# Gathered rows turned by VectorE behind a pass through DRAM, instead of by TensorE

## The chip, the cores and the metric

One Trainium2 chip; the kernel runs on one of its cores. The metric is device time in microseconds (us), the median of several executions. The engines are named as in the profile: PE is TensorE (PEld its weight loads), DVE is VectorE, ACT is ScalarE, POOL is GpSimd, SP is SyncE, which only starts DMAs here.

## What is computed

A layer in two stages over 4 x 512 tokens of width 512. The first is a state-space block; its result is added to x. The second is a mixture of experts: after a layer norm each token takes its best 6 of 16 experts, and all tokens also pass a shared one.

```python
def _swiglu(x, w13_, w2_):
    gu = x @ w13_.T
    g, u = jnp.split(gu, 2, axis=-1)
    return jax.nn.silu(g) * u @ w2_.T
...
scores = jax.nn.softmax(x @ gate_w.T, axis=-1)
topk_w, topk_ids = lax.top_k(scores, TOP_K)
topk_w = topk_w / (topk_w.sum(-1, keepdims=True) + 1e-20)
combine = jnp.einsum('tk,tke->te', topk_w, jax.nn.one_hot(topk_ids, E, dtype=topk_w.dtype))
...
out, _ = lax.scan(body, jnp.zeros_like(x), (w13, w2, combine.T))
out = out + _swiglu(x, sw13, sw2)
```

H = 512, I = 352, E = 16, TOP_K = 6; the shared expert has 2 x 352 inner columns.

## The kernel before

The program is written by hand for each engine; semaphores order the engines among each other, and each engine runs its own list in order. The first stage is left as it is but for a few constants; the second is what the change is about.

**Weights and tiles.** There are 18 weight sets of 2.2 MB: two halves of the shared expert (sets 0 and 1) and 16 experts (2 to 17). A tile is 128 tokens through one set. 32 tiles are shared ones (t < NS = 32), and here 104 routed ones follow, 6 to 7 per expert, in a loop of four tiles per turn. A routed tile's tokens are scattered rows of `token_rows`.

**Precision.** Each operand of the matmuls is taken as a high part plus a low part: `xh` is a copy of x into a narrower type, `xl = x - xh`; likewise `ah`, `al` of the middle result, and for the weights `w` (high) and w's second half (low, `wraw - w`). Three products (high x high, high x low, low x high) are summed.

**One routed tile, by engine.** `tile(t)` on PE: `up` of the chunks 0 and 1 (L1699, L1700), `turn_a(t-1)` (L1710), `up` of the chunks 2 and 3, `turn_x(t+1)` (L1687: four 128x128 transposes of the gathered rows into bank 4), `down(t-1)` (L1719). ACT: `a_high(t-1)` (L862), `x_high(t+1)` (L852, reads bank 4), `gate_up(t)` (L857), `y_out(t-1)` (L868). DVE: `a_low(t-1)` (L1399), `take_weight(t+1)` (L1372), `gather_ids(t+5)` (L1378), `x_low(t+1)` (L1363: bank 4 minus xh), `add_ids` (L1383), `multiply(t)` (L1393). POOL: `gather(t+5)` (L997), `next_weights(t)`, `expert_starts(t)`, `add(t)` (L1015, adds 128 rows into the output in DRAM). Shared tiles read rows that were stored turned, so they have no `turn_x`.

**A split.** At an expert's first tile the next set's parts are made: ACT (L822) and DVE (L1417) copy half of `wraw` each into the high part, then POOL's `split_low` (L987) subtracts all 4352 columns. The set after that is fetched by SP (L633) into the one `wraw` when L987 is done. There are 15 splits in the routed stage.

**The passage to the routed tiles.** POOL loads the token lists (L1060) after tile 26; DVE waits for them (`ids_in`) ahead of tile NS-3 = 29, where the first `gather_ids` stand (`FIRST_ROWS`).

Of the kernel before, what the change touches and what calls it, by code (L numbers as in the profile page):

```python
# [37 lines left out]
P = 128  # L38
# [24 lines left out]
SHARE = WCOLS // 2  # L63
PEELED = NS - 1
AHEAD = 5
FIRST_ROWS = {NS - 3: (NS, NS + 1), NS - 2: (NS + 2,), NS - 1: (NS + 3, NS + 4)}
# [165 lines left out]
def mamba_moe(nc, x, ctxT, g_x, g_f, inT, convw, convb, xpT, dtwT, dtb, alog, dvec,  # L232
# [4 lines left out]
    turned_d = nc.dram_tensor("token_rows_turned", (TT, P, H), F32, kind="Internal").ap()  # L237
    turned_v = turned_d.rearrange("(b c) p m -> b p c m", c=TC)
# [6 lines left out]
    with ExitStack() as ctx:  # L245
# [49 lines left out]
        dskm = alloc(mem, "dskm", [P, J, P])  # L295
# [8 lines left out]
        u1 = alloc(mem, "u1", [P, J, L])  # L304
        hs = alloc(mem, "hs", [P, 4, L])
        hc = alloc(mem, "hc", [P, 4, L])
        xlT = alloc(mem, "xlT", [P, TC, HK, P])
        szT = alloc(mem, "szT", [P, TC, H])
# [16 lines left out]
        zero = alloc(mem, "zero", [P, ROW])  # L325
# [33 lines left out]
        wraw = alloc(ctx, "wraw", [P, WCOLS])  # L359
        w = alloc(ctx, "w", [P, 4 * WCOLS], F32R)  # L360


        sg = alloc(ctx, "sg", [P, 2, I])
# [4 lines left out]
        xh = alloc(ctx, "xh", [P, 2, H], F32R)  # L368
        xl = alloc(ctx, "xl", [P, 2, H], F32R)
# [5 lines left out]
        meta = alloc(ctx, "meta", [P, 5, NT], I32)  # L375
# [13 lines left out]
        fours = alloc(ctx, "fours", [P, 2], I32)  # L389
# [57 lines left out]
        gathered = [sem(f"gathered{i}") for i in range(4)]  # L447
        zero_done = sem("zero_done")
# [31 lines left out]
        N_CONST = 10  # L480
# [30 lines left out]

        def tiles_but_12(eng):
            return eng.value_load(fours[0:1, 1:2], min_val=NS + E - 12, max_val=TILES - 12)
# [4 lines left out]
        def up_banks(t, s):  # L518

            return misc if isinstance(t, int) and t == 0 else banks[2 * s:2 * s + 2]  # L520

# [19 lines left out]
        def _(sp):  # L541
# [3 lines left out]
                      (gf, g_f.partition_broadcast(P)), (dsk, dvec.rearrange("(j p) -> p j", p=P)), (iota16, iota_d),  # L545
                      (gw, gateT.rearrange("(k p) e -> p k e", p=P))]
            sp.dma_start(ctxt[:], ctxT[bass.ds(0, 1)].rearrange("a (k p) t -> p (a k) t", p=P)).then_inc(ctx_in, 16)
            with nc.allow_non_contiguous_dma(reason="per-channel vectors of 512 values"):
                for dst, src in lead:
                    sp.dma_start(dst[:], src).then_inc(lead_in, 16)  # L550
                for dst, src in consts:
                    sp.dma_start(dst[:], src).then_inc(const_in, 16)
# [31 lines left out]
            def step(b, at):  # L584
# [7 lines left out]
                if b == NB - 1 and n == 2:  # L592
                    sp.wait_ge(dA_done, b * DS * J)
                    sp.wait_ge(g_done, b * DS)
                    sp.wait_ge(summed, (b - 1) * DS * J + J * J)
                    fetch(0)
# [33 lines left out]
            def fetch(e):  # L630

                at_least(sp, wl_done, e)
                sp.dma_start(wraw[:], wall[bass.ds(e, 1)].rearrange("a p c -> p (a c)")).then_inc(raw_in, 16)  # L633
# [24 lines left out]
            with sp.Fori(3, NX) as e:  # L658
                fetch(e)
            sp.wait_ge(meta_ready, 2)  # L660
            tiles = tiles_but_12(sp) + 12
# [5 lines left out]
        def _(act):  # L667
# [92 lines left out]
            def norm_chunk(b, t):  # L760
                act.wait_ge(nmr2_done, b + 1)
                act.wait_ge(rows_stored, 16 * (b + 1))
                nc.scalar.activation(rowb[:, t, 0:H], xrow[:, b % 2, t, :], ACT.Identity, bias=nmr2[:, t:t + 1],
# [52 lines left out]
            def split_high(e, t):  # L816
# [3 lines left out]
                apart(act, raw_in, 16 * (e + 1), "act")  # L820
                apart(act, down_done, t, "act")
                nc.scalar.copy(columns(w, (e % 2) * 2 * WCOLS, mine), wraw[:, 0:mine]).then_inc(wh_done, 1)  # L822

            def high(b, k):
                if k == 0:
                    act.wait_ge(raw_in, 16)
# [10 lines left out]
            def fetch(e):  # L837

                act.wait_ge(wl_done, e)
                act.dma_start(wraw[:], wall[bass.ds(e, 1)].rearrange("a p c -> p (a c)")).then_inc(raw_in, 16)  # L840

            def x_high(t, s):
# [5 lines left out]
                else:  # L848
                    act.wait_ge(xt_turned, t + 1)
                    source = banks[4][:]  # L850
                at_least(act, up_done, t - 1)
                nc.scalar.copy(xh[:, s, :], source).then_inc(xh_done, 1)  # L852
# [28 lines left out]
            def high_piece(e, k):  # L881
                size, base = WCOLS // EARLY, (e % 2) * 2 * WCOLS
                at = k * size
                if k == 0:
                    act.wait_ge(raw_in, 16 * (e + 1))
# [935 lines left out]
```

## Time and profile before

| | |
|---|---|
| median of 3 runs | 1438.2 us (1437.75 to 1438.47) |
| span of the profiled execution (its own time isn't given) | 1435.5 us |
| PE busy | 1349.9 us (94%) |
| POOL, DVE, ACT busy | 949.3, 787.5, 730.9 us |
| DMA | 149 MB, 104 GB/s |
| second stage | from about 490 us to the end |

The profile gives busy times per engine, the granted clock of TensorE, the chain of waits that ended last, groups of instructions by source line, and timelines. The line numbers are those of the kernel before. Matmuls overlap, so the sum of their times is more than the time that they take.

### The profile page before, as it was taken

To read this page: it belongs to the slowest core of one execution; us is meant where nothing else is said; L and a number is where in the kernel's file an instruction comes from. 1 tells how busy PE (TensorE), PEld (TensorE's weight loads), DVE (VectorE), ACT (ScalarE), POOL (GpSimd) and SP (SyncE) were. 2 spreads that over 40 slices of the span, in tenths; PEclk is the share of its full clock that TensorE was granted. 3 is DMA by queue.
4 is the path that set the end of the run, shared out by engine and by line. 5 is a ranking of instruction groups with operands and counts; after the bars stand their busy time and mean duration, and the time that the engine had idled before them with its cause. 6 is when DMAs were issued, how large, how long until landed. Compare 5 with 4: busy or idle time off the path is not lost.

```text
span 1435.5 us, 32257 instructions
## 1 busy us (share of the span) xinstructions
PE 1349.9 (94%) x8480; PEld 1210.6 (84%) x8481; DVE 787.5 (55%) x1364; ACT 730.9 (51%) x1317; POOL 949.3 (66%) x671
## 2 busy tenths in 40 slices
PE   6897998997898899999999999999999999999996
PEld 2686887887888799999998989989889988899885
DVE  6878898898989854653333333333333333333331
ACT  5898897898889464343332333323333333332321
POOL 0588898898988747887456665566645666546632
PEclk8899999999999999999999999999999999999999
DMA  4120122222242365645455435555445544454432
GB/s 137 38 74 31 53 67 96 67 73 91 75 146 72 133 129 106 142 84 141 83 141 145 131 63 144 139 147 137 104 94 137 141 135 104 95 147 131 76 68 36
DMA packets 65042, 149.13 MB, mean 104 GB/s; under 512 B 16976, under 2 KB 17616, under 8 KB 62656
## 3 DMA queue, kind: packets, MB, share of 16 engines
q0 software_dynamic: 31024, 62.10, 22.9%
q1 hardware_dynamic: 33392, 81.21, 17.5%
q10 hardware_dynamic: 560, 4.98, 1.0%
q8 instruction: 36, 0.59, 0.2%
q14 instruction: 30, 0.25, 0.1%
HBM read 101.50 MB, written 48.99 MB: 105 GB/s over the span
## 4 chain that ended last, share of the span: by engine, by line
PE 65%; DVE 3%; issue 1%; POOL 0%; ACT 0%; DVEq 0%; POOLq 0%; ACTq 0%
PE bank L1719 19%; PE bank L1699 19%; PE bank L1700 18%; PE bank L1687 3%; PE bank L1710 3%; DVE hs L1172 1%; PE bank L1604 1%; PE bank L1590 1%; PE bank L1602 0%; POOL hc L949 0%; DVE sc L1226 0%; PE bank L1665 0%; DVEq L1375 0%; DVE xl L1363 0%; DVE du L1186 0%
## 5 line engine op out<-in xcount | busy, mean ns | idle before, releaser
L949 POOL TENSOR_TENSOR hc<-hs,crow 128x512 f32<-128x512 f32 x254 | 322.6, 1302 | 91.8 <-DVE hs L1172 84.6
L1699 PE MATMUL bank<-w,xh 128*128 (+1 forms) x1088 | 368.7, 340 | 7.6 <-issue 4.2
L1015 POOL DMA_INDIRECT out_x<-ys,aid x104 | 171.2, 1646 | 275.0 <-issue 215.7
L1700 PE MATMUL bank<-w,xh 128*128 (+1 forms) x1088 | 351.2, 323 | 0.0
L1172 DVE TENSOR_TENSOR_SCAN hs<-dA,bank 128x512 f32<-128x512 f32 x256 | 295.8, 1208 | 47.9 <-PE bank L1604 32.0
L1719 PE MATMUL bank<-w,ah 128*128 (+1 forms) x816 | 264.7, 405 | 2.7 <-DVE al L1399 2.7
L1399 DVE TENSOR_TENSOR al<-bank,ah 128x384 fp32r<-128x384 f32 x136 | 75.8, 557 | 331.0 <-ACT ah L862 283.2
L1699 PEld LDWEIGHTS bank<-w,xh 128*128 128x128 f32 x1088 | 204.3, 188 | 35.9 <-issue 32.1
L1700 PEld LDWEIGHTS bank<-w,xh 128*128 128x128 f32 x1088 | 206.4, 190 | 2.3
L868 ACT COPY ys<-bank 128x512 f32<-128x512 f32 x136 | 79.9, 587 | 195.9 <-PE bank L1719 191.5
L1700 PE MATMUL bank<-w,xl 128*128 (+1 forms) x544 | 175.9, 323 | 0.0
L1699 PE MATMUL bank<-w,xl 128*128 (+1 forms) x544 | 175.7, 323 | 0.0
L1719 PEld LDWEIGHTS bank<-w,ah 128*128 128x128 f32 x816 | 145.0, 189 | 27.7 <-issue 2.2
L1590 PE MATMUL bank<-ident,hc 128*128 128x128 f32 x1024 | 160.4, 281 | 7.6 <-POOL hc L949 5.1
L862 ACT CAST ah<-bank 128x384 fp32r<-128x384 f32 x136 | 65.3, 480 | 196.9 <-PE bank L1710 166.7
L786 ACT ACTIVATE dA<-delta,aneg 128x512 f32<-128x512 f32 x256 | 164.0, 710 | 0.0
L1604 PE MATMUL bank<-bdiag,duT 128*128 128x128 f32 x1024 | 163.7, 285 | 0.0
L1719 PE MATMUL bank<-w,al 128*128 (+1 forms) x408 | 161.2, 395 | 0.0
L852 ACT CAST xh<-bank 128x512 fp32r<-128x512 f32 x104 | 61.2, 588 | 182.9 <-PE bank L1687 175.4
L987 POOL TENSOR_TENSOR w<-wraw,w 128x4352 f32 x15 | 143.8, 9588 | 0.7 <-issue 0.5
L1604 PEld LDWEIGHTS bank<-bdiag,duT 128*128 128x128 f32 x1024 | 142.5, 201 | 0.0
L1590 PEld LDWEIGHTS bank<-ident,hc 128*128 128x128 f32 x1024 | 124.3, 145 | 11.0 <-POOL hc L949 6.7
(184 smaller groups left out, 2051.7 us busy)
## 6 DMA issues: line engine op xcount, KB each, us to landing
wraw<-in_wall SPq DMA_DIRECT2D x16, 2176.0 KB
crow<-c_rows SPq DMA_DIRECT2D x64, 256.0 KB, 3.3
xt<-token_rows_turned SPq DMA_DIRECT2D x32, 256.0 KB
out_x<-ys POOLq DMA_DIRECT2D x32, 256.0 KB
wraw<-in_wall ACTq DMA_DIRECT2D x2, 2176.0 KB
token_rows<-rowb SPq DMA_DIRECT2D x4, 1028.0 KB
xrow<-in_x SPq DMA_DIRECT2D x4, 1024.0 KB, 7.0
out_x<-xrow SPq DMA_DIRECT2D x4, 1024.0 KB, 4.9
```

The lines of the kernel that those rows point to most:

```text
L786: nc.scalar.activation(dA[:, 4 * (n % 2) + j, :], delta[b % 2][:, j, :], ACT.Exp, scale=aneg[:, j, n:n + 1]).then_inc(dA_done, 1)
L868: nc.scalar.copy(ys[:, slot, :], banks[7][:]).then_inc(ys_done, 1)
L949: nc.gpsimd.tensor_tensor(hc[:, j, :], hs[:, j, :], crow[:, n % 4, :], ALU.mult).then_inc(hc_done, 1)
L987: nc.gpsimd.tensor_tensor(columns(w, at + WCOLS, WCOLS), wraw[:], columns(w, at, WCOLS), ALU.subtract).then_inc(wl_done, 1)
L1015: pool.indirect_dma_start(out_rows, bass.IndirectOffsetOnAxis(ap=aid[:, s:s + 1], axis=0), ys[:, s, :], None, bounds_check=TOKENS - 1, oob ...
L1172: nc.vector.tensor_tensor_scan(hs[:, j, :], dA[:, 4 * (n % 2) + j, :], dbu[j % 2][:], 0.0, ALU.mult, ALU.add).then_inc(scanned, 1)
L1399: nc.vector.tensor_tensor(al[:, s, :], banks[5][:, 0:IP], ah[:, s, :], ALU.subtract).then_inc(al_done, 1)
L1590: mm = nc.tensor.matmul(ysum[t][:, cols], hc[:, j, t * P:(t + 1) * P], ident[:], start=n == 0 and j == 0, stop=n == DS - 1, is_transpose=T ...
L1604: mm = nc.tensor.matmul(dbu[j % 2][:, t * P:(t + 1) * P], duT[b % 2][:, t, j * P:(j + 1) * P], bdiag[:, n % 2, t - COPIED, :], start=True, ...
L1699: nc.tensor.matmul(gate_bank[:, 0:I], xx, columns(w, off + ww + k * 2 * I, I), start=first, stop=last)
L1700: mm = nc.tensor.matmul(up_bank[:, 0:I], xx, columns(w, off + ww + k * 2 * I + I, I), start=first, stop=last)
L1719: mm = nc.tensor.matmul(banks[7][:], aa, columns(w, off + ww + W2AT + k * H, H), start=k == 0 and n == 0, stop=k == IK - 1 and n == 2)
```

## The change

- A routed tile's rows, gathered into `xt` as before, are stored to DRAM (`gathered_rows`) by SP, 256 KB, and read back by SP in four DMAs, one for each quarter of the partitions: partition 32q + r of `xq` gets, for each of four groups of 32 tokens, 128 columns (512 B) of a token.
- DVE's STREAM_TRANSPOSE (`turn_x`, first in its tile) turns each 32x32 block of `xq` into `xsq`; `x_high` and `x_low` read `xsq`, blockwise, where they read bank 4. PE's `turn_x` is gone.
- So that blocks fall where the matmuls want them, the normed rows are written in another order of columns, and the sets 0 and 1 and the gate's weights are loaded in that order (five and four DMAs instead of one).
- `wraw` has two halves. From set 4 on a set is fetched by ACT's queue, right behind ACT's copy of the set before (`fetch_after`), where SP waited for L987.
- The first gathers stand one tile earlier: from tile NS-4 = 28 on, with the wait for `ids_in`.
- SP stores a tile's rows one tile ahead of reading back: store of t+1, then the four reads of t.

```diff
-FIRST_ROWS = {NS - 3: (NS, NS + 1), NS - 2: (NS + 2,), NS - 1: (NS + 3, NS + 4)}
+FIRST_ROWS = {NS - 4: (NS, NS + 1), NS - 3: (NS + 2,), NS - 2: (NS + 3,), NS - 1: (NS + 4,)}
+ROWS_FROM = min(FIRST_ROWS)
...
+            def bounce_out(t, s, m=None):
+                rows_in(sp, t, s, m, "sp")
+                apart(sp, xt_turned, t - 3, "sp")
+                sp.dma_start(bounce_d[s], xt[:, s, 0:H]).then_inc(bounced[s], 16)
+            def bounce_in(t, s, m=None):
+                apart(sp, bounced[s], 16 * ((t - NS) // 4 + 1) if isinstance(t, int) else 16 * m + 16, "sp")
+                apart(sp, xt_turned, t - 3, "sp")
+                for q in range(NQ):
+                    sp.dma_start(xq[q * Q:(q + 1) * Q, s, :].rearrange("r (g f) -> r g f", g=NQ), quarter_v[s, q]).then_inc(quartered[s], 16)
...
-            with sp.Fori(3, NX) as e:
-                fetch(e)
+            fetch(3)
             sp.wait_ge(meta_ready, 2)
+            groups = routed_groups(sp)
+            bounce_out(NS, 0)
+            with sp.Fori(0, groups - 1) as i:
+                for k in range(4):
+                    t = 4 * i + NS + k
+                    bounce_out(t + 1, (k + 1) % 4, i + (k + 1) // 4)
+                    bounce_in(t, k, i)
...
+            def fetch_after(e, t):
+                apart(act, wl_done, e, "act")
+                late = act.value_load(meta[0:1, 5, bass.ds(t, 1)], min_val=0, max_val=NX - 1)
+                act.dma_start(columns(wraw, ((e + 1) % 2) * WCOLS, WCOLS),
+                              wall[bass.ds(late, 1)].rearrange("a p c -> p (a c)")).then_inc(raw_in, 16)
...
                 with act.If(e > 0):
                     split_high(e, t)
+                    fetch_after(e, t)
...
-                    apart(pool, xt_turned, t - 3, "pool")
+                    apart(pool, bounced[s], 16 * ((t - NS) // 4 if isinstance(t, int) else before), "pool")
...
+            def turn_x(t, s4, m=None):
+                if isinstance(t, int) and t < NS:
+                    return
+                quarters_in(dve, t, s4, m, "dve")
+                apart(dve, xl_done, t, "dve")
+                nc.vector.transpose(xsq[:], xq[:, s4, :]).then_inc(xt_turned, 1)
...
-                source = xt[:, t % 4, 0:H] if isinstance(t, int) and t < NS else banks[4][:]
-                nc.vector.tensor_tensor(xl[:, s, :], source, xh[:, s, :], ALU.subtract).then_inc(xl_done, 1)
+                if isinstance(t, int) and t < NS:
+                    nc.vector.tensor_tensor(xl[:, s, :], xt[:, t % 4, 0:H], xh[:, s, :], ALU.subtract).then_inc(xl_done, 1)
+                else:
+                    dve.wait_ge(xt_turned, t + 1)
+                    nc.vector.tensor_tensor(xl[:, s, :].rearrange("p (c g r) -> p c g r", c=NQ, r=Q),
+                                            xsq[:].rearrange("p (g c r) -> p c g r", g=NQ, r=Q),
+                                            xh[:, s, :].rearrange("p (c g r) -> p c g r", c=NQ, r=Q), ALU.subtract).then_inc(xl_done, 1)
...
                 s = s4 % 2
+                turn_x(t + 1, (s4 + 1) % 4, m)
                 a_low(t - 1, 1 - s)
...
-                if t == NS - 3:
+                if t == ROWS_FROM:
                     dve.wait_ge(ids_in, 16)
...
-                if more and not (isinstance(t, int) and t + 1 < NS):
-                    turn_x(t + 1, (s4 + 1) % 4, m)
```

VectorE, one routed tile in the loop, behind the split's branch; before (cc is the token's weight, gid the next gather's indices):

```order
L1399 TENSOR_TENSOR al<-bank,ah 128x384
...
L1372 COPY cc<-xt 128x1
...
L1378 COPY gid<-lists 128x1
L1360 REGISTER_ALU
L1363 TENSOR_TENSOR xl<-bank,xh 128x512
```

and in the change (its own line numbers):

```order
L1450 STREAM_TRANSPOSE xsq<-xq 128x512
L1497 TENSOR_TENSOR al<-bank,ah 128x384
...
L1470 COPY cc<-xt 128x1
...
L1476 COPY gid<-lists 128x1
L1453 REGISTER_ALU
L1459 TENSOR_TENSOR xl<-xsq,xh 128x512
```

The transpose stands ahead of al, and x_low, at its old place behind gid, reads xsq where it read a bank.

SyncE behind the last shared rows; before:

```order
L658 UNCONDITIONAL_BRANCH
L633 ISA
L633 DMA wraw<-in_wall 128x4352
L658 REGISTER_ALU
L658 COMPARE_AND_BRANCH
```

and in the change, the first two tiles of the loop's turn:

```order
L684 DMA gathered_rows<-xt 128x512
L720 UNCONDITIONAL_BRANCH
L720 ISA
L500 ISA
L684 DMA gathered_rows<-xt 128x512
L500 REGISTER_ALU
L691 DMA xq<-gathered_rows 32x4x128 x4
L500 REGISTER_ALU
L684 DMA gathered_rows<-xt 128x512
L691 DMA xq<-gathered_rows 32x4x128 x4
```

The fetches of weights have left the loop; the reads of a tile stand behind the store of the next one.

## Rows read from the trace of the kernel before

**Rows 1.** The page's first line.

```profile
span 1435.5 us, 32257 instructions
```

**Rows 2.** Busy time by engine in a window: PE, PEld, DVE, ACT, POOL; clock, DMA share, GB/s.

```profile
450.00:1400.00 950.00, 936.22 (x5548) 856.23 (x5548) 396.34 (x893) 344.12 (x617) 586.09 (x381) 1.00 0.50 118
```

**Rows 3.** The chain in order of time (start, us, what): two shared, then routed tiles.

```profile
644.05 0.33 PE bank L1710 x3
...
650.35 0.33 PE bank L1710 x3
...
677.78 2.09 PE bank L1719 x9
...
722.55 0.33 PE bank L1710 x3
...
729.29 0.33 PE bank L1710 x3
```

**Rows 4.** TensorE's line 1687: count, ns min/median/max, first and last start.

```profile
L1687 PE MATMUL bank<-ident,xt x416: 270/272/273, 697.0 to 1410.1; 128*128 128x128 f32 x139
```

**Rows 5.** Timeline of DVE: an ordinary tile's al; then a split's gid and x_low.

```profile
1006.54 0.56 DVE L1399 TENSOR_TENSOR al<-bank,ah 128x384 fp32r<-128x384 f32 x1 [2.24 <-ACT ah L862]
...
1023.06 0.15 DVE L1378 COPY gid<-lists 128x1 int32 x1 [0.68 <-issue]
1023.24 0.69 DVE L1363 TENSOR_TENSOR xl<-bank,xh 128x512 fp32r<-128x512 f32 x1
```

**Rows 6.** Timeline of POOL in the same split, and the gather behind it.

```profile
1022.79 9.58 POOL L987 TENSOR_TENSOR w<-wraw,w 128x4352 f32 x1
...
1034.44 0.99 POOL L997 DMA_INDIRECT xt<-token_rows,gid  x1 [0.30 <-issue]
```

**Rows 7.** Lines 1150, 1363 and 987, columns as in rows 4.

```profile
L1150 DVE TENSOR_TENSOR delta<-delta,du x16: 681/1080/1769, 27.6 to 365.1; 128x512 f32<-128x512 f32 x16
...
L1363 DVE TENSOR_TENSOR xl<-bank,xh x104: 690/692/693, 698.2 to 1411.1; 128x512 fp32r<-128x512 f32 x104
...
L987 POOL TENSOR_TENSOR w<-wraw,w x15: 9564/9587/9625, 711.1 to 1342.3; 128x4352 f32 x15
```

**Rows 8.** Timelines of DVE and POOL around one of the 16 L1150.

```profile
119.64 1.42 DVE L1150 TENSOR_TENSOR delta<-delta,du 128x512 f32<-128x512 f32 x1
...
119.25 1.27 POOL L949 TENSOR_TENSOR hc<-hs,crow 128x512 f32<-128x512 f32 x1
```

**Rows 9.** Timelines: x_low of the first, ninth and last split; POOL's L987 of the ninth.

```profile
712.23 0.69 DVE L1363 TENSOR_TENSOR xl<-bank,xh 128x512 fp32r<-128x512 f32 x1
...
1071.92 0.69 DVE L1363 TENSOR_TENSOR xl<-bank,xh 128x512 fp32r<-128x512 f32 x1
...
1342.96 0.69 DVE L1363 TENSOR_TENSOR xl<-bank,xh 128x512 fp32r<-128x512 f32 x1
...
1072.21 9.59 POOL L987 TENSOR_TENSOR w<-wraw,w 128x4352 f32 x1
```

**Rows 10.** Timeline of PE: the first up matmul behind that split.

```profile
1024.96 0.43 PE L1699 MATMUL bank<-w,xh 128*128 x1 [0.64 <-issue]
```

**Rows 11.** Windows as in rows 2: an idle TensorE, and what follows.

```profile
440.70:445.40 4.70, 0.00 (x0) 0.00 (x0) 4.56 (x16) 4.70 (x10) 2.04 (x2) 1.00 0.24 52
445.60:448.90 3.30, 3.30 (x16) 3.30 (x17) 2.17 (x2) 3.29 (x4) 3.30 (x3) 0.50 0.00 1
```

**Rows 12.** Timelines of POOL and DVE at tile 28.

```profile
678.11 0.59 POOL L1060 DMA_DIRECT2D lists<-token_lists  x1 [0.47 <-DMA token_lists<-ids,posi]
...
676.40 0.56 DVE L1399 TENSOR_TENSOR al<-bank,ah 128x384 fp32r<-128x384 f32 x1 [3.79 <-issue]
```

**Rows 13.** DMA issues: count, KB each, median us to landing; one issue of SP's.

```profile
lists<-token_lists POOLq DMA_DIRECT2D x1, 136.0 KB, 3.8
...
ones<-in_ones_d SPq DMA_DIRECT2D x1, 64.0 KB, 2.7
...
25.56 0.43 SPq L628 DMA_DIRECT2D ones<-in_ones_d  x1
```

More of the change, by code:

```diff
@@ L388, in mamba_moe @@
         lasti = alloc(ctx, "lasti", [P, 1], I32)
-        fours = alloc(ctx, "fours", [P, 2], I32)
+        fours = alloc(ctx, "fours", [P, 3], I32)
+        xq = alloc(ctx, "xq", [P, 4, H])
+        xsq = alloc(ctx, "xsq", [P, H])
         lead_in = sem("lead_in")
@@ L447, in mamba_moe @@
         gathered = [sem(f"gathered{i}") for i in range(4)]
+        bounced = [sem(f"bounced{i}") for i in range(4)]
+        quartered = [sem(f"quartered{i}") for i in range(4)]
         zero_done = sem("zero_done")
@@ L479, in mamba_moe @@
         N_WARM = 4
-        N_CONST = 10
+        N_CONST = 13
         N_PLAN = 7
@@ L520, in up_banks, with raw_of, raw_count, load_raw @@
             return misc if isinstance(t, int) and t == 0 else banks[2 * s:2 * s + 2]
+        def raw_of(e):
+            return 0 if isinstance(e, int) and e < 3 else (e % 2) * WCOLS
+        def raw_count(e):
+            return 16 * (NQ + 1) * (e + 1) if isinstance(e, int) and e < 2 else 16 * e + 16 * (2 * NQ + 1)
+        def load_raw(eng, e):
+            into = columns(wraw, raw_of(e), WCOLS)
+            if e > 1:
+                eng.dma_start(into, wall[e]).then_inc(raw_in, 16)
+                return
+            parts = wall[e][:, 0:W2AT].rearrange("(q r) (c m) -> c r q m", r=Q, c=NQ)
+            for c in range(NQ):
+                eng.dma_start(into[c * Q:(c + 1) * Q, 0:W2AT].rearrange("r (q m) -> r q m", q=NQ), parts[c]).then_inc(raw_in, 16)
+            eng.dma_start(into[:, W2AT:WCOLS], wall[e][:, W2AT:WCOLS]).then_inc(raw_in, 16)
+        def by_part(a):
+            return a.rearrange("p (q c r) -> p c q r", q=NQ, r=Q)
         def split(e, k, pieces):
@@ L657, in _ @@
                 x_load(t)
-            with sp.Fori(3, NX) as e:
-                fetch(e)
+            fetch(3)
             sp.wait_ge(meta_ready, 2)
+            groups = routed_groups(sp)
[5 more added lines that the diff above has]
+                    bounce_in(t, k, i)
+            rest, rounds = tiles_but_12(sp) + 8, groups_but_2(sp) + 1
+            for k in range(4):
+                if k < 3:
+                    bounce_out(rest + k + 1, k + 1, rounds)
+                bounce_in(rest + k, k, rounds)
             tiles = tiles_but_12(sp) + 12
@@ L1065, in _ @@
                     t = 4 * i + NS + k
-                    gather(t + AHEAD, (k + AHEAD) % 4)
+                    gather(t + AHEAD, (k + AHEAD) % 4, i + (k + AHEAD) // 4)
                     next_weights(t)
@@ L1725, in weights_of, with tile @@
                 apart(pe, wl_done, needed, "pe")
-                return pe.value_load(meta[0:1, 1, bass.ds(t, 1)], min_val=0, max_val=2 * WCOLS)
-            def tile(t, s4, old, off, more=True, m=None):
+                return pe.value_load(meta[0:1, 1, bass.ds(t, 1)], min_val=0, max_val=4 * WCOLS)
+            def tile(t, s4, old, off):
                 s = s4 % 2
@@ L1769, in of_last @@
             def of_last(k):
-                return pe.value_load(meta[0:1, 1, bass.ds(last - k, 1)], min_val=0, max_val=2 * WCOLS)
-            tile(last, 3, lambda: of_last(1), weights_of(last), False)
+                return pe.value_load(meta[0:1, 1, bass.ds(last - k, 1)], min_val=0, max_val=4 * WCOLS)
+            tile(last, 3, lambda: of_last(1), weights_of(last))
             turn_a(last, 1)
```

105 lines of the change are left out of this document (61 added, 44 removed).

## The prediction

> **What bounds the kernel now.** Look first at the busy times of the routed stage: from 450 to 1400 us TensorE works 936 of 950 us, at a granted clock of 1.00, while VectorE has work for 396 us, ScalarE for 344 and GpSimd for 586 [rows 2]. So the second stage is TensorE's, and an instruction taken off it counts in full, as long as nobody comes late. Then the chain in order of time: a shared tile, which turns no rows on TensorE, takes 650.35 - 644.05 = 6.30 us; a routed tile, which does, takes 729.29 - 722.55 = 6.74 [rows 3]. The difference, 0.44 us, is what the four transposes of line 1687 cost on the path; there are 416 of them, 104 tiles' worth [rows 4]. Third, the timeline of VectorE and GpSimd around one split (the step in which a new expert's weights become a high and a low part): GpSimd's subtraction L987 runs from 1022.79 for 9.58 us, and VectorE's x_low L1363 starts at 1023.24, under it, and still takes 0.69 [rows 5, 6]. It reads a bank and xh. That row carries the prediction.
>
> The profiled execution spans 1435.5 us [rows 1]; its own time is not on the page, and the runs' median of 1438.2 is 2.7 above the span. I put these 2.7 around the changed span too, so sums start from 1438.2. A difference of 0.2%, 2.9 us, is about what can be told from no change here.
>
> **The change, part by part.**
>
> *TensorE's transposes go.* 104 x 0.44 = 45.8 us off the path.
>
> *The turning on VectorE comes.* One STREAM_TRANSPOSE of 128x512 per routed tile, ahead of al. No such row exists; al takes 0.56 and x_low 0.69 [rows 5], so I take 0.65, between half and twice that. It stands where VectorE sits idle 2.24 us before al [rows 5]: nothing on the path, at 1.3 us neither. If a quarter lands late this cover turns into a wait, and al, x_low and then TensorE's down are queued behind it (rivals).
>
> *x_low changes its inputs.* It now reads xsq and xh, both in SBUF. Take VectorE's delta L1150, which also reads two SBUF tensors. Alone it takes 0.68 us; among GpSimd's multiplications up to 1.77 [rows 7]. Case by case: GpSimd's L949 runs 119.25 to 120.52, L1150 starts at 119.64 inside it and ends at 121.06, 0.54 after GpSimd's end [rows 8]. I went through the 11 that began inside a GpSimd multiplication: each ends about 0.55 after that one's end and none earlier. The x_low of before never pays this: 690 to 693 ns in all 104 [rows 7], with a bank as its other input. So the new x_low, if it starts under L987, waits for L987's end. It does: in the first split x_low starts at 712.23 and L987 at 711.1, in the last at 1342.96 and 1342.3; in 14 of 15 x_low is 0.4 to 1.2 us behind. Only the one at 1071.92 is ahead of its L987, by 0.29 [rows 7, 9]. The change doesn't bring x_low forward, since it starts right behind gid, not behind TensorE's turning (gid from 1023.06, x_low from 1023.24 [rows 5]), and L987 starts right behind a gather in both kernels. Price: L987 ends at 1032.37, x_low 0.55 later at 1032.92; the tile's first matmul, at 1024.96 before [rows 10] and 0.44 earlier without the turning, starts at about 1032.97. That is 8.45 us; in the first split the same working gives 8.1. I take 8.4, so 14 x 8.4 = 117.6. In the fifteenth the next tile's x_low is held instead, for the last 3 us: 3. Sum 120.6. Behind it all stand multiply, TensorE's up and everything of the next tile; nothing else fills TensorE.
>
> The longest wait that a row shows is 1.77 - 0.68 = 1.09 us, behind an instruction of 1.27; whether it also lasts 9 us behind one of 9.58, no row shows. Bounds: 1.1 us, of which x_low's spare hides most (it ended at 1023.93, 0.6 us ahead of the moved-up matmul), and the full remainder. I take the full one, because all the ends follow GpSimd's end and none its start. The Trainium skill ("SBUF — State Buffer", section "SBUF: two separate sides") has a rule on exactly this: VectorE with two SBUF inputs and a GpSimd instruction that reads SBUF share a pair of ports, and whichever starts first has it "for the whole instruction". By that rule each split pays the full remainder, as in my sum; with a hold of 1.1 us at most, 15 splits would cost about 8 us and the kernel would stand at rival 2.
>
> *The clock.* After an idle TensorE of 440.7 to 445.4 the granted clock was 0.50 from 445.6 to 448.9 [rows 11], the lower of its two levels (1.2 against 2.4 GHz), and half of these 3.4 us is lost: 1.7. An idle of 8 us per split has no row; I take 1.7 for each of the 14 (bounds 0 and 2.8): 23.8.
>
> *The first gathers move one tile forward.* VectorE now waits for ids_in ahead of tile 28. The load of lists is issued at 678.11 and lands 3.8 later, at 681.9; tile 28's al stood at 676.40 [rows 12, 13]. It slips by 5.5, to an end at 682.6, and down, which started at 677.78 [rows 3], by 4.8: with what follows al I take 5 us, once, and 1.7 of clock.
>
> *The way through DRAM.* 104 x (256 KB out, 256 KB back): 512 KB per tile beside DMA engines that are busy half of the time [rows 2]. SyncE issues five DMAs per tile at 0.43 each [rows 13], 2.2 us in a period of 6.3. In a tile without a split this all fits into the lead of the gathers; costed at nothing. The cover is two tiles of lead. The other weight sets come by ScalarE's queue right behind its copy, with GpSimd's subtraction still to run, so about 10 us earlier than SyncE's (which waited for L987): nothing on the path. The five pieces of set 0 and 1 and three more constants are issued while those queues wait anyway: nothing.
>
> **Sum:** 1438.2 - 45.8 + 120.6 + 23.8 + 6.7 = 1543.5; I say 1543. This case's own range: 13 full holds of 8.1 and no loss of clock, 1438.2 - 45.8 + 5 + 105 + 6 = 1508; 15 of 8.5 with 2.8 of clock each, 1438.2 - 45.8 + 7 + 170 = 1570.
>
> **Rivals.**
>
> 1. *x_low slips in front of the subtraction.* If the wait for a tile's turning is gone and VectorE gets 0.4 to 1.2 us ahead, all splits go like the one at 1071.92: the next tile's x_low waits about 3 us, with 1.7 of clock. 1438.2 - 40.8 + 15 x 4.7 = 1468. Against it: x_low hangs on gid, whose place is unchanged.
>
> 2. *The hold is short, and the kernel is faster.* What decides then is the gather behind a split. It is issued at 1034.44, since GpSimd was in L987 until 1032.37 [rows 6]. Landing as the lists do, 3.8, gives 1038.2; the pieces of the tile before are issued only behind this tile's store (SyncE's order), so the last of four starts 1.8 later and lands 2.7 after that, as `ones`, the same 512 B per partition, did [rows 13]: 1042.7. Turning, al and down (0.65 + 0.56 + 2.1 [rows 3], with 0.1 between) put the next tile at 1046.1; it was due three periods behind 1024.52, at 1043.4. So 2.7 us per split, 40 in all, which cancels 45.8 - 5. The kernel is faster by more than a measurement needs only if the pieces land before about 1042.5. With the four landing 3.3 behind the gather instead of 4.5, the splits cost 1.5 each: 1438.2 - 40.8 + 22 = 1420. For it: nothing shows a 9.6 us hold. Against: no row shows VectorE let in before GpSimd's end.
>
> 3. *The hold is short and the pieces are late*, by the traffic they add: 4 us per split, 1438.2 - 40.8 + 60 = 1457. About equal, if the estimate of rival 2 holds as it stands.
>
> **How the numbers follow.** Forecast 0.80, rival 1 0.06, rival 2 0.07, rival 3 0.07 (0.03 of it within 0.2%). The time is the forecast's. From 1465 to 1575 the range takes in rival 1 and nearly all of the forecast's own 1508 to 1570; rivals 2 and 3, 0.14, stay out with a few hundredths of tails. Faster 0.07, same 0.03, slower 0.90.
>
> **What would show it.** Right: x_low with a mean far over 0.69, 14 or 15 of them near 9.5 us, each ending 0.5 us after a subtraction; no turning on TensorE and 6.3 us per tile elsewhere; in each split an idle TensorE of 8 us ended by x_low, the clock at 0.5 after it; one wait of 5 us at tile 28. Wrong: x_low at 0.7 throughout (then look for VectorE's turning waiting for quarters five tiles into each expert, and TensorE idle before down), or a clock that stays at 1.0, which alone would bring the time to about 1518.

## The result, and the profile after

The changed kernel takes 1583.1 us (median of 4 runs, 1580.2 to 1584.8) against 1438.0 for the kernel before beside it: a ratio of 1.102, 95% interval 1.100 to 1.103. The forecast was 1543, its range 1465 to 1575. Its direction and its main mechanism hold; the time lies 8 us outside.

The first lines to read are the page's: the span, VectorE's x_low with a mean of 1922 ns where all 104 took 0.69 before [rows 7], and up's first line, ahead of which TensorE idled 141.9 us, 131.6 of it ended by x_low.

```profile
span 1578.4 us, 32970 instructions
...
L1792 PE MATMUL bank<-w,xh 128*128 (+1 forms) x1088 | 387.4, 357 | 141.9 <-DVE xl L1459 131.6
...
L1459 DVE TENSOR_TENSOR xl<-xsq,xh 128x512 fp32r<-128x512 f32 x104 | 199.9, 1922 | 5.9
```

The window that answers to [rows 2] is 140 us longer, and TensorE has no more to do in it: 938 us in 1090, at a granted clock of 0.93.

```profile
450.00:1540.00 1090.00, 938.05 (x5127) 842.25 (x5127) 589.62 (x992) 347.58 (x617) 585.43 (x381) 0.93 0.60 155
```

Now a split, in the timelines of VectorE, GpSimd and TensorE. x_low (L1459) starts 1.14 us behind the subtraction and ends at 1100.67, 0.56 behind the subtraction's end (1100.11); multiply, TensorE's up and all else stand behind it.

```profile
1091.62 0.15 DVE L1476 COPY gid<-lists 128x1 int32 x1 [0.69 <-issue]
1091.84 8.83 DVE L1459 TENSOR_TENSOR xl<-xsq,xh 128x512 fp32r<-128x512 f32 x1
...
1090.70 9.41 POOL L1069 TENSOR_TENSOR w<-wraw,w  x1
...
1100.90 0.66 PE L1792 MATMUL bank<-w,xh 128*128 x1 [8.04 <-DVE xl L1459]
```

In all 15 splits x_low takes 8.51 to 10.08 us and ends 0.55 or 0.56 behind the subtraction; TensorE's 15 idles there sum to 126.0 us (7.75 to 9.18). The windows behind that split (columns as in [rows 2]) show the clock at its lower level, 0.50 and 0.51, from 1095.7 to 1106, over the rest of the idle and the first 5.1 us of work after it (1.60 + 3.50); from 1106 to 1112 it is at 1.00.

```profile
1095.70:1102.50 6.80, 1.60 (x5) 1.60 (x6) 6.14 (x4) 0.00 (x0) 6.33 (x3) 0.50 0.48 145
1102.50:1106.00 3.50, 3.50 (x14) 3.43 (x14) 0.00 (x0) 0.47 (x2) 0.91 (x1) 0.51 0.83 149
```

An ordinary routed tile stands next (VectorE, then TensorE). From one turn_a (L1803) to the next such a tile takes 6.74 us in the median, without any turning on TensorE.

```profile
1055.65 0.56 DVE L1497 TENSOR_TENSOR al<-bank,ah 128x384 fp32r<-128x384 f32 x1 [1.27 <-ACT ah L942]
1056.62 0.15 DVE L1470 COPY cc<-xt 128x1 f32 x1 [0.41 <-issue]
1058.11 0.15 DVE L1476 COPY gid<-lists 128x1 int32 x1 [1.34 <-issue]
1058.32 0.69 DVE L1459 TENSOR_TENSOR xl<-xsq,xh 128x512 fp32r<-128x512 f32 x1
...
1059.31 0.43 PE L1792 MATMUL bank<-w,xh 128*128 x1 [0.17 <-issue]
```

And tile 28, in the chain in order of time: the lists' load, al, down.

```profile
678.45 3.20 DMA lists<-token_lists
...
681.98 0.57 DVE al L1497
682.59 3.91 PE bank L1812 x9
```

A tile's length is read from one start of turn_a to the next in TensorE's timeline (L1710 before, L1803 after). Over the routed stage that gives the whole difference (one such step per tile; a split's step is the one in which its subtraction starts):

| part | before | after | difference | forecast |
|---|---|---|---|---|
| 15 tiles with a split | 7.46 each | 16.80 each | +140.1 | +137.8 (120.6 + 23.8 - 15 x 0.44) |
| tile 28 | 6.29 | 12.49 | +6.2 | +6.7 |
| the 90 other steps | 615.3 in all | 611.5 | -3.8 | -39.2 (89 x 0.44) |
| sum | | | +142.5 (spans: +142.9) | +105.3 |

So the splits came about as forecast, and the gain did not come. Of the 90 other steps 15 are the next behind a split (101.3 us in all before, 106.0 after); the 75 that are left, the ordinary steps below, went from 514.0 to 505.5, a mean of 6.85 and 6.74. Two questions were left: is it really the hold, and why is a tile without transposes no shorter?

### The profile page after: what moved, and what is told of

It reads as the page before. It is cut to its first block, busy times and chain, and to the rows that moved or that the text cites. A ratio compares the mean times of both kernels' runs of the same rounds, so it can differ in the third digit from the quotient of the medians.

```text
span 1578.4 us, 32970 instructions
## 1 busy us (share of the span) xinstructions
PE 1356.9 (86%) x8064; PEld 1199.0 (76%) x8065; DVE 981.7 (62%) x1470; ACT 734.6 (47%) x1317; POOL 949.2 (60%) x671
## 4 chain that ended last, share of the span: by engine, by line
PE 45%; DVE 12%; issue 5%; DVEq 4%; POOL 4%; ACTq 2%; ACT 2%; DMA 0%; POOLq 0%
PE bank L1792 14%; PE bank L1793 13%; PE bank L1812 12%; DVE xl L1459 9%; POOL token_lists L1109 3%; PE bank L1803 2%; DVEq L1473 2%; DVEq L1467 1%; DVE hs L1255 1%; ACT ah L942 1%; PE bank L1704 1%; PE bank L1690 1%; POOL out_x L1091 1%; ACTq L897 0%; PE bank L1702 0%
## 5 line engine op out<-in xcount | busy, mean ns | idle before, releaser
L1792 PE MATMUL bank<-w,xh 128*128 (+1 forms) x1088 | 387.4, 357 | 141.9 <-DVE xl L1459 131.6
L1793 PE MATMUL bank<-w,xh 128*128 (+1 forms) x1088 | 362.7, 334 | 0.0
L1792 PEld LDWEIGHTS bank<-w,xh 128*128 128x128 f32 x1088 | 216.5, 199 | 186.6 <-issue 184.2
L1812 PE MATMUL bank<-w,ah 128*128 (+1 forms) x816 | 259.0, 399 | 7.6 <-DVE al L1497 7.3
L1793 PEld LDWEIGHTS bank<-w,xh 128*128 128x128 f32 x1088 | 215.7, 198 | 1.4
L1459 DVE TENSOR_TENSOR xl<-xsq,xh 128x512 fp32r<-128x512 f32 x104 | 199.9, 1922 | 5.9
L1792 PE MATMUL bank<-w,xl 128*128 (+1 forms) x544 | 181.3, 333 | 0.0
L1793 PE MATMUL bank<-w,xl 128*128 (+1 forms) x544 | 181.2, 333 | 0.0
L1812 PEld LDWEIGHTS bank<-w,ah 128*128 128x128 f32 x816 | 150.1, 189 | 36.0 <-issue 6.3
L1069 POOL TENSOR_TENSOR w<-wraw,w x15 | 140.9, 9393 | 0.5 <-issue 0.2
```

The source lines that it names most:

```text
L1069: nc.gpsimd.tensor_tensor(columns(w, at + WCOLS, WCOLS), columns(wraw, raw_of(e), WCOLS), columns(w, at, WCOLS), ALU.subtract).then_inc(wl ...
L1459: nc.vector.tensor_tensor(xl[:, s, :].rearrange("p (c g r) -> p c g r", c=NQ, r=Q), xsq[:].rearrange("p (g c r) -> p c g r", g=NQ, r=Q), x ...
L1792: nc.tensor.matmul(gate_bank[:, 0:I], xx, columns(w, off + ww + k * 2 * I, I), start=first, stop=last)
L1793: mm = nc.tensor.matmul(up_bank[:, 0:I], xx, columns(w, off + ww + k * 2 * I + I, I), start=first, stop=last)
L1812: mm = nc.tensor.matmul(banks[7][:], aa, columns(w, off + ww + W2AT + k * H, H), start=k == 0 and n == 0, stop=k == IK - 1 and n == 2)
```

## The experiments

All times are medians; the kernel before, measured beside each, was at 1435.9 to 1437.8, and every ratio is to it. Where an expectation speaks of the first run, that is the one with the turned rows in a bank; the third is the one with x_low ahead of gather_ids, the fourth has both. "Tile behind the split" is the next step after the split's own, 7.07 us in the changed kernel.

**The hold alone, in the kernel before.**

```
-                source = xt[:, t % 4, 0:H] if isinstance(t, int) and t < NS else banks[4][:]
+                source = xt[:, t % 4, 0:H] if isinstance(t, int) and t < NS else blank[:]
```

> The kernel before the change, with one operand of x_low moved: in routed tiles it subtracts xh from a blank tile in SBUF (zeros) instead of from the bank, so the low part of x is left out of what is computed; size, place and everything else stay. This is the hold alone, without the way through DRAM and without ScalarE's weight queue. Lead theory (two SBUF inputs shut out by GpSimd's 9.6 us subtraction): x_low at 8 to 10.5 us in all 15 splits, each split 8.5 to 9.5 us longer, so 1437 + 128 to 143 = 1565 to 1580 us. Rival (in the changed kernel the hold hid behind, or was made by, late rows, and by itself costs little): under 1500.

Measured 1588.2 us, ratio 1.105 (1.103 to 1.107). Line 1364, the moved x_low (duration ns min/median/max, then who waited for it):

```profile
L1364 DVE TENSOR_TENSOR xl<-blank,xh x104: 691/693/10218, 698.3 to 1562.6; 128x512 fp32r<-128x512 f32 x104
...
  PE bank L1701: 128.1, 15
```

Fifteen waits, 128.1 us; the split's step is 17.11, 9.65 more than before. The time is 8 us above the expected range, x_low's 8.78 to 10.22 us are within theirs. One operand's place makes a loss as large as the whole change's, with no other part of it. The lead theory stands.

**The turned rows in a bank.** STREAM_TRANSPOSE writes PSUM bank 4, which x_high and x_low read.

```
-                nc.vector.transpose(xsq[:], xq[:, s4, :]).then_inc(xt_turned, 1)
+                nc.vector.transpose(banks[4][:], xq[:, s4, :]).then_inc(xt_turned, 1)
```

> Only the place of the turned rows changes: VectorE's STREAM_TRANSPOSE writes PSUM bank 4, so x_low has one SBUF input again. Lead theory (x_low with two SBUF inputs is shut out for the whole of GpSimd's 9.4 us subtraction): x_low takes 0.69 to 0.72 us in all 104 tiles, the tile behind a split falls from 16.8 to 6.5 to 8.5 us, and with 15 splits at 8.3 to 10 each less the time falls by 125 to 150, to 1433 to 1458 us; ordinary tiles stay at 6.7. Rival (the 9 us at a split come from something else that the change brought there, the way through DRAM or ScalarE's weight DMA behind its copy): the splits stay at 14 us or more, and the time above 1550.

Measured 1502.9, ratio 1.046 (1.044 to 1.047). x_low is free again in all tiles, and the split's step is 7.18. But only 80 us came back, not 140: the tile behind the split went from 7.07 to 11.13 (15 x 4.06 = 61). The lines of x_low and of STREAM_TRANSPOSE with what VectorE waited for, the chain at one such tile, and ScalarE's weight DMA:

```profile
L1459 DVE TENSOR_TENSOR xl<-bank,xh x104: 690/692/694, 705.5 to 1478.0; 128x512 fp32r<-128x512 f32 x104
...
L1450 DVE STREAM_TRANSPOSE bank<-xq x104: 714/726/729, 701.0 to 1473.7; 128x512 f32<-128x512 f32 x104
...
  DMA xq<-gathered_rows: 144.3, 52
...
1109.58 9.24 DMA xq<-gathered_rows
...
1108.39 0.36 ACTq L897 DMA_DIRECT2D wraw<-in_wall  x1
```

Quarters issued 1.2 us behind a weight set took 9.2 us to land. In the changed kernel VectorE waited 11.2 us for quarters in 10 places, here 144.3 in 52: the hold had hidden a second wait.

**The subtraction in eight pieces.**

```
+                for k in range(8):
+                    c = k * (WCOLS // 8)
+                    low = nc.gpsimd.tensor_tensor(columns(w, at + WCOLS + c, WCOLS // 8), ...
```

> Only GpSimd's subtraction changes: eight instructions of 544 columns instead of one of 4352. Lead theory (x_low waits for the end of the GpSimd instruction in whose run it starts): no x_low takes more than about 2.5 us (one piece of 1.2 us, twice at most, and 0.7), the tile behind a split falls from 16.8 to about 8 to 9 us, and the time by 15 x 8, to 1455 to 1485. Rival 1 (VectorE is let in only when GpSimd's whole row of instructions is through): x_low stays at 8.5 us or more at the splits, the time at 1575 to 1595. Rival 2 (it is not this sharing at all): also no change.

Measured 1589.9, ratio 1.106 (1.104 to 1.108): rival 1. GpSimd's eight pieces (one row here) and x_low:

```profile
1096.39 10.35 POOL L1071 TENSOR_TENSOR w<-wraw,w  x8
...
1096.50 10.79 DVE L1462 TENSOR_TENSOR xl<-xsq,xh 128x512 fp32r<-128x512 f32 x1
```

VectorE was not let in between back-to-back instructions in 14 splits; in the first one it was, behind one piece (x_low 1.15 us). Nor do instructions in a row always shut it out: in the first stage of the kernel before, 10 of the 11 L1150 that began inside a multiplication were let in at its end, though the next one followed at once. The one behind [rows 8] took 1.72 us in place of 1.27:

```profile
120.47 1.72 POOL L949 TENSOR_TENSOR hc<-hs,crow 128x512 f32<-128x512 f32 x1
```

What differs isn't shown. The rows show this much: in the 14 splits GpSimd's gather ends 0.03 us or less ahead of the first piece, in the first split 0.29 us.

**x_low ahead of gather_ids.**

```
-                elif gathers:
-                    gather_ids(t + AHEAD, (s4 + 1) % 4)
                 x_low(t + 1, 1 - s)
+                if gathers:
+                    gather_ids(t + AHEAD, (s4 + 1) % 4)
```

> Only VectorE's order in a routed tile changes: x_low goes ahead of gather_ids (a register load and the gid copy, some 1.5 us), whose result GpSimd needs a tile later. Lead theory (the tile without the turning on TensorE is bound by VectorE's row al, cc, register load, gid, x_low): x_low ends 1 to 1.5 us earlier, ordinary routed tiles fall from 6.7 to 6.3 us, some 75 to 88 of them, 31 to 37 us in all. At the splits x_low then starts ahead of GpSimd's subtraction in many cases, and the next tile's is held for its last 1 to 3 us: 15 x 5 to 8 less. In all 1583 - 34 - 100 = 1450, between 1420 and 1490; if x_low still starts behind the subtraction, 1525 to 1550. Rival (the tile is held at 6.7 by rows that land or are turned late): tiles stay at 6.7 and the gain, if any, comes from the splits alone.

Measured 1576.6, ratio 1.093 (1.086 to 1.100). Both halves of the expectation missed. At the splits x_low now starts ahead of the subtraction and is held all the same:

```profile
1092.00 10.58 DVE L1459 TENSOR_TENSOR xl<-xsq,xh 128x512 fp32r<-128x512 f32 x1
...
1092.65 9.37 POOL L1069 TENSOR_TENSOR w<-wraw,w  x1
```

Twelve that started 0.37 to 0.66 us ahead lost; one that started 0.15 ahead took 0.69, and there the subtraction took 9.95; one was through before the subtraction began, and one began behind it. In all twelve GpSimd's gather was still running when x_low began, and the subtraction followed it within 0.03 us; where 0.15 was enough (the first split again) GpSimd was idle for 0.48 us ahead of the subtraction. A gather alone held none: 60 other x_low beside one took 0.69 to 0.71. And ordinary steps stayed at 6.75 in the median, though x_low ends early. VectorE's x_low, then TensorE:

```profile
1064.60 0.69 DVE L1459 TENSOR_TENSOR xl<-xsq,xh 128x512 fp32r<-128x512 f32 x1
...
1067.14 0.43 PE L1792 MATMUL bank<-w,xh 128*128 x1 [0.23 <-issue]
```

TensorE still idles 0.23 us, 1.85 us after x_low. So something of TensorE's own stands there. Its sequencer's rows name it: two loads of a register per tile (weights_of), which come behind down's wait for al. In the changed kernel (PEldq is the sequencer; count, ns min/median/max, first and last start):

```profile
L1817 PEldq TENSOR_LOAD <-meta x105: 297/385/933, 697.5 to 1554.2; - x105
...
L1819 PEldq TENSOR_LOAD <-meta x105: 294/302/591, 698.4 to 1555.1; - x105
```

That gives a round of waits for one tile: turn_a, a_high, al, the loads, up's first two chunks, the next turn_a. Medians over the ordinary tiles of the changed kernel: 1.60 us from turn_a's start to al's end, 3.10 to the next up, 2.04 to the next turn_a, 6.74 in all. In the kernel before they are 1.60, 3.20 and 2.00, 6.80 in all; in the tile whose al stands in [rows 5], al ends at 1007.10 and the next up starts 3.38 us later:

```profile
1010.48 0.43 PE L1699 MATMUL bank<-w,xh 128*128 x1
```

Beside the middle part TensorE had the transposes and down to work on before, and has only down now, but the round is as long.

**Both rows of register loads.** Three kernels with the turned rows in the bank: x_low ahead of gather_ids; TensorE's two values for the next tile read early, ahead of turn_a and of down, in three tiles of four; and both.

```
                 up(t, s, (0, 1), off)
+                if needed_next:
+                    needed_next()
                 turn_a(t - 1, 1 - s)
...
                 up(t, s, (2, 3), off)
+                if offset_next:
+                    offset_next()
```

> The changes of the first and the third run together: turned rows in bank 4, and x_low ahead of gather_ids. Lead theory (hold at the splits and VectorE's order in the tile are what took the gain): x_low 0.7 us everywhere, ordinary tiles 6.3, splits 6.5 to 8, so 1583 - 140 - 36 = 1407, between 1395 and 1430, which is below the kernel before the change (1438). Rival (the pieces that come through DRAM arrive late behind each split, 1.5 to 4.5 us each, as worked out from the kernel before): 1430 to 1470, with VectorE's STREAM_TRANSPOSE waiting for quarters some five tiles into each expert.

> The first run (bank 4) and TensorE's early register values, without the move of x_low. If VectorE's row (al, cc, register load, gid, x_low, which ended 4.39 us behind the start of turn_a) is a second limit of the same length, ordinary tiles stay at 6.6 to 6.75 and the time at 1493 to 1503 us; if TensorE's register values were the only limit, this comes out as the run with both, at 1470 to 1480.

> The fourth run (bank 4, x_low ahead of gather_ids) and one thing more: TensorE reads the next tile's two register values (expert and weight offset) ahead of turn_a and of down, in three tiles out of four; the first tile of each four reads them where it did. What is to be told apart is why ordinary routed tiles stay at 6.7 us though x_low now ends more than 1 us earlier. Theory A (TensorE's queue stands at down until al is there, and only then reads the registers for the next tile, 2.8 to 3.1 us from the end of al to the next matmul, where 2.1 us of down is the only work): three of four ordinary tiles fall to 6.3, one stays at 6.6 to 6.7, 75 tiles by about 0.3 to 0.4, so 1470 to 1480 us. Theory B (the limit is something else, such as ScalarE or the DMA): all stay near 6.7, 1495 to 1505.

Measured 1501.5, 1508.0 and 1505.6 (ratios 1.044, 1.050, 1.047, each to within 0.002): no gain in time in any, and all three outside the ranges expected (the one with both by 0.6 us). But the tiles tell the causes apart. Of 105 steps, 6.36 us or less took: in the bank kernel 0, with x_low moved 0, with TensorE's values early 18, with both 39. Four starts of turn_a in a row in the one with both, 6.30 and 6.31 apart:

```profile
1126.58 0.49 PE L1803 MATMUL bank<-ident,am 128*128 128x128 f32 x3
...
1132.88 0.49 PE L1803 MATMUL bank<-ident,am 128*128 128x128 f32 x3
...
1139.19 0.49 PE L1803 MATMUL bank<-ident,am 128*128 128x128 f32 x3
...
1145.50 0.49 PE L1803 MATMUL bank<-ident,am 128*128 128x128 f32 x3
```

TensorE's loads are the first limit, VectorE's row the second. The time did not follow since the rows come no faster: with both, VectorE waits 156.3 us for quarters, in 60 places.

**The same in the changed kernel, hold and all**, where rows have time to catch up at each split; TensorE's loop turns over in the middle of a tile, so all four tiles read early.

```
+                    turn_a(t - 1, 1 - s)
+                    needed = pe.value_load(meta[0:1, 0, bass.ds(t + 1, 1)], min_val=1, max_val=NX)
+                    up(t, s, (2, 3), off)
+                    following = offset_of(t + 1)
+                    down(t - 1, 1 - s, old)
+                    apart(pe, wl_done, needed, "pe")
+                    up(t + 1, 1 - s, (0, 1), following)
```

> The changed kernel with nothing done against the hold (turned rows stay in SBUF), but with both register moves: x_low ahead of gather_ids, and TensorE's register values for the next tile read while it has work queued, in all four tiles. The hold gives the rows 9 us of extra lead at each split, so here the supply of rows should not stand in the way. If the two rows of register loads are what kept ordinary tiles at 6.7 us, most of the 74 tiles between the splits fall to 6.31 to 6.4: 1583 - 74 x 0.35 = 1557 us, between 1545 and 1565, or less where an x_low slips by the subtraction. If the supply of rows limits them even behind a hold, tiles of 6.31 stand beside tiles of 7 and more, with VectorE waiting for quarters in more than 30 tiles, and the time stays above 1568.

Measured 1555.0, ratio 1.080 (1.077 to 1.082): 28 us less, as expected, but not from the ordinary tiles alone. In two of the 15 splits of the profiled execution x_low slipped by (steps of 6.95 and 7.07), as in two of the run with x_low moved alone; together with the steps behind them the splits give 12.6 us. The 75 ordinary steps give 15.5: 490.0 us in all, median 6.37 (6.74 in the changed kernel). Forty of the 105 steps are at 6.36 or less (none there). The round is now 1.60 + 2.80 + 1.94 = 6.34. Against the run with x_low moved alone (1576.6), in which the same two splits were free, TensorE's loads are the only difference, and they give 21.6 us. VectorE waits 44.0 us for quarters in 35 places, the sign of a short supply of rows, so that is no longer wholly out of the way. From the kernel before, the 75 ordinary steps now gain 24.0 of the 33 us that 75 x 0.44 would be: this is where most of the gain went.

**The rows' way through DRAM.** Four kernels on the bank kernel. First, the weight set as two DMAs of four strided pieces, so 2176 B in a row in place of 17408:

```
+                for h in range(2):
+                    act.dma_start(into[:, :, h, :], source[:, :, h, :]).then_inc(raw_in, 16)
```

> The first run (turned rows in bank 4) and one thing more: a weight set is fetched by two DMAs of rows cut into four pieces of 544 columns, so packets of 2176 B in place of 17408 B; bytes, queue and place are the same. What is to be told apart is why the tile two behind a split took 9.4 to 13.5 us (mean 11.1) there, with VectorE's STREAM_TRANSPOSE waiting for quarters that were issued about 9 us before. Theory A (the quarters' 512 B packets each stand behind a 0.65 us packet of the weight set on the same DMA engine): that tile falls to 7 to 8.5 us, the time by 15 x 2.5 to 4, to 1440 to 1465 us. Theory B (the gather is late because GpSimd was in its subtraction, and the pieces follow it, as worked out from the kernel before): the tile stays at 10 us or more and the time at 1495 to 1510.

Measured 1489.9, ratio 1.036 (1.032 to 1.039). ScalarE's queue (queue, packets, MB, share) went from the first row (the bank kernel) to the second:

```profile
q10 hardware_dynamic: 3296, 38.41, 7.1%
```

```profile
q10 hardware_dynamic: 16976, 38.41, 7.6%
```

The tile behind the split fell from 11.13 to 7.49, so theory A holds for that tile (a row of 17408 B takes 0.65 us in the median, one of 512 B 0.03). But the time fell by 13, not by 38 or more: two and more tiles later others took 8 to 13.6 us, and VectorE still waited 131.9 us for quarters. The wait moved on. Second, SyncE's order:

```
-                    bounce_out(t + 1, (k + 1) % 4, i + (k + 1) // 4)
+                    bounce_out(t, k, i)
                     bounce_in(t, k, i)
```

> The first run (bank 4) and one thing more: SyncE's order. It now writes tile t's gathered rows to DRAM and reads the same tile's quarters back right after, where it wrote tile t+1's rows first, so that the quarters of a tile were issued only when the next tile's rows had landed, a tile later. If the rows' supply lacks lead (gather 4.7 us, out 2.1, one tile of 6.7 lost in SyncE's order, quarters 4, against 4 tiles less GpSimd's 9.5 us), these 4 to 5 us per tile bring the tile two behind a split from 11.1 to 6.8 to 8.5 us: 1503 - 15 x 2.6 to 4.3 = 1438 to 1464. If it is the long weight packets alone, the quarters land late all the same: that tile stays at 9.5 or more and the time above 1480.

Measured 1483.0, ratio 1.032 (1.030 to 1.035): the tile behind the split at 9.10 on the mean (6.4 to 13.6), between both expectations, and the time above 1480, on the second one's side. Third and fourth, the combinations:

> All together: bank 4, x_low ahead of gather_ids, TensorE's early register values, weight packets of 2176 B, and the first gathers back at the tiles of the kernel before. Lead theory (the hold, the two rows of register values, the long weight packets and the wait for ids_in are the whole of the difference): 1502 - 54 - 25 - 6 = 1417 us, between 1400 and 1440, with tile 28 at 6.3 to 7 us; the kernel before is at 1437. If the quarters of the first gathers come late when these start a tile later, tiles 31 and 32 show it with 1 to 6 us. Rival: the remaining costs at the splits keep it at 1450 or more.

> All that the runs so far point to: bank 4, x_low ahead of gather_ids, SyncE's order as in the run beside this one, weight packets of 2176 B, and TensorE's register values for the next tile read while it has work queued, in all four tiles (its loop now turns over in the middle of a tile); the first gathers stay where the change put them. If rows then come in time, ordinary tiles are at 6.31 to 6.4 us (6.7 now) and the splits at 6.5 to 8: 1503 - 60 - 75 x 0.4 = 1413 us, between 1395 and 1435, below the kernel before the change. If the supply of rows by way of DRAM limits the kernel even so, tiles of 6.31 stand beside tiles of 7 to 9 with VectorE waiting for quarters, and the time stays above 1450.

Both missed their ranges on the side of the rivals. The one with the first gathers moved back (1493.1, ratio 1.039, 1.037 to 1.041) has tile 28 at 6.31, and then two steps of 12.5 and 12.8 us at 31 and 33, where the first rows are late: the move forward had its reason. The other is the fastest of the changed kernels, 1463.9, ratio 1.018 (1.017 to 1.020), and still slower than before. Its chain from 900 to 1300 us, by line:

```profile
by line: DMA gathered_rows<-xt 25.5%; PE bank L1814 12.0%; issue 9.7%; SPq L693 9.6%; DMA xq<-gathered_rows 9.3%; PE bank L1794 7.3%; PE bank L1795 6.8%; DMA xt<-token_rows,gid 6.3%; POOL w L1071 2.9%; DMA out_x<-ys,aid 2.2%; PE bank L1805 
```

With that order SyncE's own turn (from a write to DRAM to the first read 4.3 us, then four issues, 1.8; medians) is nearly as long as a tile of 6.3. No version of the way through DRAM that I tried beats the kernel before; more slots for rows in flight was not tried.

**Did the loads limit the kernel before?** The same early values there, the transposes left on TensorE: in all four tiles, in all four with x_low moved too, and in three of four with the loop as it was.

> The kernel before the change, with one thing moved: TensorE's register values for the next tile are read while it has work queued (its loop turns over in the middle of a tile), the transposes still on TensorE. Between the splits its tiles took 6.88 us on the mean, where their work is 6.74, and TensorE stood idle 36 us ahead of up in 83 places with nothing but its register loads beside it. If these loads already limited the kernel before, ordinary tiles fall to 6.74 and the time by 100 x 0.1 to 0.16 us and part of the splits' 0.7: 1437 - 12 to 25, 1412 to 1427 us, below both kernels. If they were covered there, the time stays within 3 us of 1437.

> The run beside this one, and x_low ahead of gather_ids as well. In the kernel before x_low ended 0.6 us ahead of need, so the move should give nothing where the register loads are out of the way: within 4 us of the run beside it. If VectorE's row limits once TensorE's loads are covered, this one is 5 us or more faster, with more tiles at 6.74.

> The kernel before, with TensorE's register values for the next tile read early in three tiles out of four, and its loop left to turn over where it did. In the run with all four, two tiles of four stood at 6.74 and two at 7.3 to 7.9, since the loop's own two loads had come to stand where TensorE had nothing queued. Here the first tile of four keeps its loads where they were (about 6.9 to 7.0 us), the other three should be at 6.74: 1437 - 75 x 0.1 = 1428 to 1434 us, just below both kernels. If the early loads themselves leave TensorE idle, tiles stay above 6.85 on the mean and the time at 1437 or more: then the loads were covered in the kernel before, as far as they can be.

Measured 1462.2, 1466.1 and 1437.5 (ratios 1.016, 1.020 and 1.0002; the last from 0.9992 to 1.0013). The first missed: two steps of four stand at 6.74, the other two at 7.3 to 7.9, where the loop's own loads now stand with nothing queued on TensorE (13.5 us of idle ahead of turn_a, in 26 places, one per turn). The second is within 4 us of it, as expected. The third tells more: two ordinary steps of four went to 6.74 and 6.73 on the mean (from 6.82 and 6.89), but the other two to 7.01 and 7.08 (from 6.91 and 6.79), so the mean is 6.89, and was 6.85. In the kernel before none of these moves gave time back. That another place for the loads would give a little there is not excluded.

## Why the prediction was wrong, point by point

**The step that failed is the first one: "104 x 0.44 = 45.8 us off the path".** The 0.44 came from a shared tile of 6.30 beside a routed one of 6.74 [rows 3], as if the transposes were the only difference. They are not: a shared tile's weights and rows have fixed places, while a routed tile reads two registers on TensorE between al and the next up, and one on VectorE between cc and gid. The round from turn_a by way of al and the loads to the next turn_a was 6.80 us in the kernel before and is 6.74 without the transposes, since they stood beside the loads and not in the round. Without them an ordinary tile waits for the loads instead (6.74 us on the mean, from 6.85); with the loads and x_low moved, it takes 6.53. Of 39.2 us outside the splits 3.8 came; that is 35 of the 40 that the forecast was short. The busy 936 of 950 us [rows 2] said that TensorE had work all the time; it did not say that taking 0.44 away would leave nothing else 0.4 us behind.

**The hold: right.** In the changed kernel x_low with two SBUF inputs waits out the whole subtraction, 15 of 15, as worked out from GpSimd's much shorter instructions [rows 8]; moving one operand costs 152 us by itself, moving it back frees x_low wholly. Forecast 8.4 us of idle, measured 8.40 on the mean and 8.04 in the split above. Rival 1 fell: the one x_low that began ahead (0.15) took 10.08. With it fell the forecast's own fifteenth split, which was to cost 3 us. The Trainium skill ("SBUF — State Buffer", section "SBUF: two separate sides") says that whichever of the two starts first has the ports "for the whole instruction". The trace agrees on the length of one instruction (9.4 us). Two things the runs show beyond it or otherwise, and there they decide: eight instructions in a row can hold x_low as one does (10.79 us, 14 of 15 splits), and by the rows' starts the first doesn't always win: an x_low whose row begins 0.65 us ahead lost, with a gather of GpSimd's running.

**The clock: right in size.** At half clock TensorE worked 5.1 us behind the split shown. That step took 16.43; less 8.04 of idle and 6.3 of work at full clock, some 2.1 us were lost (an estimate), for 1.7 forecast, inside the bounds of 0 to 2.8. The sum over the splits, 140.1 for 137.8, is nearer than its parts: hold and clock cost some 13 us more than forecast, while the 0.7 us by which a split's step exceeded an ordinary one before (7.46 to 6.74) went away beside the hold, about 11 in all.

**Tile 28: right**, 6.2 for 6.7.

**"The way through DRAM costs nothing": right for this kernel only.** Its cover was the hold. Once that goes, the tile behind each split waits 4.1 us, where rivals 2 and 3 had worked out 2.7 to 4. That the size agrees is in part luck: they had counted the late gather and the traffic, but not the long rows of the weight set, and with short rows 3.6 of the 4.1 were gone from that tile. Rival 2's faster kernel was not to be had: with the hold away and nothing else, 1503, and with all the moves that I tried, 1464.

**The range** ended at 1575. The case that it lacked is no gain from the transposes: 1543 + 40.

## What to carry to other kernels

Before you book an instruction's time as gain, ask what else would end last if it were gone, and look for it in the sequencers' rows too: register loads show no engine busy. Give an elementwise instruction on VectorE that runs beside a long GpSimd one an operand in PSUM. And when a large wait goes, expect the next one to be among the costs that it covered: here 61 of 140 us came back as late rows.

## What was not expected of the hardware

GpSimd's back-to-back instructions kept VectorE out as one would, in 14 splits of 15: x_low 10.79 us beside eight of about 1.3. In the first stage VectorE was let in between two of them. A VectorE row that began 0.37 to 0.66 us ahead of GpSimd's lost, 12 times of 12. Rows of 512 B took 9.2 us to land beside a weight set with rows of 17408 B, and with rows of 2176 B that tile went from 11.13 to 7.49. One register load of TensorE's sequencer took 0.29 to 0.93 us, and two of them stand in each routed tile. STREAM_TRANSPOSE of 128x512 f32 took 0.71 us into SBUF and 0.73 into PSUM.
